# At most two of the first scatter's stores on their way, where four were allowed

## The reference

```python
xn = _layernorm(x)
x = x + _L0_gnn_ref(xn, edge_index, edge_weight, ...) + _L0_mix_ref(xn[None], ...)[0]
x = x + _L0_ffn_ref(_layernorm(x)[None], ...)[0]
xn = _layernorm(x)
x = x + _L1_gnn_ref(xn, src, dst, deg_isqrt[:, None], ...) + _L1_mix_ref(xn[None], ...)[0]
x = x + _L1_ffn_ref(_layernorm(x)[None], ...)[0]
```

## Time and profile before

| What | us |
|---|---|
| median of the timed runs | 6407.51 |
| span of the recorded execution, first to last instruction | 7249.7 |
| TensorE (PE) busy in it | 5328.2 |
| GpSimd (POOL) busy in it | 3860.9 |
| GpSimd, the 1564 stores of both scatters | 1589.6 |
| GpSimd, the 1760 gathers | 1718.7 |

### The profile page before, as it was taken

How to read it: one execution, slowest core, us unless ns; L and a number is a source line. 1 busy time by engine, 2 the same in 40 slices (tenths; PEclk the granted TensorE clock), 3 DMA queues, 4 the chain that set the end, 5 groups by cost and what they waited for, 6 DMA issues and landing times.

```text
span 7249.7 us, 87859 instructions
## 1 busy us (share of the span) xinstructions
PE 5328.2 (73%) x24977; PEld 4445.0 (61%) x24977; DVE 3382.5 (47%) x9891; ACT 1308.8 (18%) x2962; POOL 3860.9 (53%) x4349
## 2 busy tenths in 40 slices
PE   0111110667659999999899999979999899997794
PEld 0000000556537777777678887868788778876682
DVE  8511100666645555555464464436444554446323
ACT  0000000111101111111142242214111231111240
POOL 0777776000055555555888888830666326654205
PEclk9755555778779999999999999989999999999895
DMA  1000000221133333335310011021333223353223
GB/s 37 9 12 12 12 12 11 73 66 58 59 105 98 96 99 100 98 97 93 49 48 18 14 40 34 20 70 48 91 95 97 76 71 107 108 93 109 89 94 117
DMA packets 319771, 477.56 MB, mean 66 GB/s; under 512 B 99008, under 2 KB 240054, under 8 KB 319470
## 3 DMA queue, kind: packets, MB, share of 16 engines
q0 software_dynamic: 153136, 262.81, 14.8%
q1 hardware_dynamic: 166334, 211.17, 9.5%
HBM read 371.27 MB, written 102.33 MB: 65 GB/s over the span
## 4 chain that ended last, share of the span: by engine, by line
PE 57%; another core or an unknown queue 13%; DVE 11%; issue 11%; DMA 4%; DVEq 2%; ACT 1%; SPq 1%; POOL 1%; ACTq 0%; POOLq 0%
PE bank L2277 13%; PE bank L2288 13%; PE bank L2505 5%; PE bank L2338 5%; PE bank L2487 4%; PE bank L2323 4%; PE bank L2774 3%; PE bank L2630 2%; PE bank L2268 2%; PE bank L2816 1%; DMA sb_work_QT<-scratch_q 1%; DMA sb_rows<-scratch_xn,sb_row_of 1%; DMA sb_work_XC<-in_x 1%; DVE sb_STATE L1391 1%
## 5 line engine op out<-in xcount | busy, mean ns | idle before, releaser
L995 POOL DMA_INDIRECT sb_rows<-scratch_xn,sb_row_of x1760 | 1718.7, 977 | 1553.2 <-PE bank L2323 619.1
L988 POOL DMA_INDIRECT scratch_sorted<-sb_FREE x1564 | 1589.6, 1016 | 546.5 <-issue 379.2
L2288 PE MATMUL bank<-sb_work_FT,sb_W 128*128 128x250 f32 x4400 | 1006.9, 380 | 19.6 <-ACT sb_work_FT L1075 15.1
L2288 PEld LDWEIGHTS bank<-sb_work_FT,sb_W 128*128 128x128 f32 x4400 | 845.3, 193 | 134.6 <-ACT sb_work_FT L1075 22.0
L1075 ACT ACTIVATE sb_HT<-bank,sb_cols 128x250 f32<-128x250 f32 x1333 | 552.8, 467 | 2047.2 <-PE bank L2487 811.6
L2277 PE MATMUL bank<-sb_W,sb_HT 128*125 128x256 f32 x4000 | 894.2, 380 | 1.1 <-ACT sb_HT L1075 1.1
L2277 PEld LDWEIGHTS bank<-sb_W,sb_HT 128*125 128x125 f32 x4000 | 752.7, 188 | 115.4 <-ACT sb_HT L1075 1.9
L2277 PE MATMUL bank<-sb_W,sb_work_FT 128*125 128x256 f32 x1600 | 409.3, 406 | 449.8 <-issue 378.3
L2277 PEld LDWEIGHTS bank<-sb_W,sb_work_FT 128*125 128x125 f32 x1600 | 315.0, 201 | 518.0 <-issue 450.5
L2323 PE MATMUL bank<-sb_rows,sb_work_TM 128*125 128x257 f32 x1760 | 444.8, 392 | 91.2 <-issue 29.7
L1660 DVE TENSOR_TENSOR sb_FREE<-sb_FREE,bank 125x257 f32 x440 | 186.1, 423 | 698.0 <-PE bank L2323 455.1
(11 more groups left out here) (375 smaller groups left out, 7606.2 us busy)
## 6 DMA issues: line engine op xcount, KB each, us to landing
sb_rows<-scratch_xn,sb_row_of POOLq DMA_INDIRECT x1760
scratch_sorted<-sb_FREE POOLq DMA_INDIRECT x1564
scratch_qT<-sb_work_QF SPq DMA_DIRECT2D x100, 250.0 KB
sb_work_QF<-scratch_qT SPq DMA_DIRECT2D x100, 250.0 KB
sb_work_XC<-in_x SPq DMA_DIRECT2D x50, 250.0 KB
sb_work_ZT<-scratch_xn SPq DMA_DIRECT2D x50, 250.0 KB
sb_W<-in_L_mix_W SPq DMA_DIRECT2D x9, 1024.0 KB
sb_work_XC<-scratch_zs SPq DMA_DIRECT2D x28, 256.0 KB, 2.6
```

The source lines that it names most:

```text
L988: nc.gpsimd.indirect_dma_start(out=sorted_d[e], out_offset=bass.IndirectOffsetOnAxis(ap=pos[e][0:n, c:c + 1], axis=0), in_=rec[e][0:n, 2 * ...
L995: nc.gpsimd.indirect_dma_start(out=rows[:, t % RING, 0:D], out_offset=None, in_=table, in_offset=bass.IndirectOffsetOnAxis(ap=row_of[:, t: ...
L2288: ins = nc.tensor.matmul(dst[:, b, :], w[:, k0 + k, 128 * (b0 + b):128 * (b0 + b) + 128], source[:, k, :], start=(n == 0), stop=(n == 2 * ...
```

## The change

The limit becomes one for each scatter: two stores on their way in scatter 0, four in scatter 1. The semaphores that are counted up and the counts that are waited for follow from it. `PACED` stays 0.

```diff
 PACED = 0
 FLYING = 4
+FLYING_OF = (2, FLYING)
...
         def all_scattered(e):

-            return [(scattered[e][h], 16 * ((EC - h + FLYING - 1) // FLYING)) for h in range(FLYING)]
+            n = FLYING_OF[e]
+            return [(scattered[e][h], 16 * ((EC - h + n - 1) // n)) for h in range(n)]
...
-                if c >= FLYING:
-                    pool.wait_ge(scattered[e][c % FLYING], 16 * (c // FLYING))
+                if c >= FLYING_OF[e]:
+                    pool.wait_ge(scattered[e][c % FLYING_OF[e]], 16 * (c // FLYING_OF[e]))
...
-                    in_=rec[e][0:n, 2 * c:2 * c + 2], in_offset=None).then_inc(scattered[e][c % FLYING], 16)
+                    in_=rec[e][0:n, 2 * c:2 * c + 2], in_offset=None).then_inc(scattered[e][c % FLYING_OF[e]], 16)
```

## The result

The changed kernel takes 6607.34 us (median of 4 runs, 6603.01 to 6620.09), the kernel before 6406.42 us on the same chip: a ratio of 1.0311, 95% interval 1.0296 to 1.0325. It is 200.9 us slower. The forecast said slower by 72 us with a range up to 6570, so the sign was right and the size was not.

What follows compares the result with a forecast made beforehand. The later of B0's end and scatter 0's end, plus what follows, was taken as the bound. 70 delayed stores (88 us) less 10 us already waited made 78; less slack, 72: 6407.5 + 72 = 6480 us, range 6385 to 6570.

Steps and rivals of the forecast that it cites:

- The stall is the recording's: Phase A0: 854.8 us of stall in SP's loads belong to the recording; timed runs take about 27 us a pair.
- Scatter 0 ends with B0, at some 1162 to 1175 us: Before the expert weights' issue: scatter 0 ends with B0 or some us behind it, so its delay shows.
- It costs nothing in quiet stretches: Scatter 0 without traffic beside it: waiting for the store two places ahead adds no time, 1.263 us a store.
- the 1.56: Scatter 0 at limit two: 1.56 us from the end of the store two ahead to a store's own start.
- the rival in which every store waits: Scatter 0: semaphores rise late in quiet stretches too, so all stores wait; slower, 6575 us, chance 0.08.
- 120 us and half of 78: Sum behind 6575 us: 120 us for waits of all stores, on top of half of the traffic's cost.
- A store beside traffic lands 2.18 us after its end: Scatter 0 beside 100 GB/s or more: landing time taken from the first gather, giving 1.65 us a store.
- 376 us of traffic, 70 stores left over, 10 us of waits at four already: A0 and B0: 298 stores fit at 1.263 us, 228 at 1.65; 88 us less 10, net 78 us.
- Hidden anyway: Scatter 0 ends well before B0 in timed runs, so its delay falls into the gap; same, 6407 us, chance 0.23.
- Stores yield: A0 beside scatter 0: fewer stores give the loads back some 36 us; faster, 6372 us, chance 0.22.
- The recorded span of about 7265 us: Profiled run of the changed kernel: only some six pairs of A0 beside the scatter, so 15 us longer.

Runs made afterwards that it cites:

- e4: Changed kernel with a limit of eight instead of two stores on their way in scatter 0: 6333.55 us, ratio 0.9892 to the kernel before.
- e1: Changed kernel with limit four and the last 280 of scatter 0's 782 stores left out: 6274.56 us, ratio 0.9804 to the kernel before.
- e8: The kernel before, unchanged at limit four, recorded a second time: median 6411.55 us, recorded span 6409.8 us.
- e5: Changed kernel, limit two, SP's 125-partition transfers in A0 and B0 split at partition 112: 6443.45 us, ratio 1.0047 to the kernel before.

## Why the prediction was wrong

*The stall is the recording's.* Right. Two further recordings have pairs of 27.6 us beside the stores, against the 169.4 us of the earlier trace rows and the 26.93 that I took.

*Scatter 0 ends with B0, at some 1162 to 1175 us.* Wrong, and this is the first step that failed: 6407.5 - (7249.7 - 2016.7) = 1174.5, "if all behind it runs as recorded". It didn't run as recorded. From the issue of the expert weights to the end the first recording took 5233.0 us, the second one 6409.8 - 1314.64 = 5095.2. These 138 us too much put the point 138 us too early. Of them 119 lie behind the first gather (7249.7 - 2042.87 = 5206.8 against 6409.8 - 1322.21 = 5087.6); why is open. The other 19 are VectorE's work between B0 and the gathers, which the scatter hides when it ends last. The agreement that I trusted, 854.8 us of stall against 842.2 us of difference, came about by chance: the recording had the 138 us more, and lacked the 153 us for which SP waits for scatter 0 behind B0 in a timed run, because its scatter was hidden.

I had also worked out 1242 from the recorded mean pace, and passed over it. In e4, where no store waits for another, the last store starts at 1242.9; the waits at four add 69 us, which makes the 1311.6 of the kernel before. e1 shows the slip by itself: 128 us to be had at four.

*It costs nothing in quiet stretches.* Right: 1.29 us a store behind B0 at a limit of two, where the median from issue to landing is 2.1 us, that is 1.1 us after the store's end and within the 1.56. That excludes the rival in which every store waits, though its 6575 us lies nearer to the result than my forecast. (Its terms, 120 us and half of 78, give 6566.)

*A store beside traffic lands 2.18 us after its end.* Wrong, and this is the mis-sized term: 5.25 us in the mean of the five stores that were waited for beside the pair shown. I had the right row: the store of the earlier trace rows that landed 6.2 us after its end was an ordinary one. I set it aside since only four waits were recorded. But a limit of four lets a landing of up to 4 x 1.263 - 0.96 = 4.1 us pass without a wait, and few transfers stood beside that scatter (11 GB/s from 260 to 600 us, where the second recording has 74); rare waits said nothing of the landing. The gather of the earlier trace rows was no stand-in. The 125 GB/s that I put beside it are the mean of a stretch of 100 us. While it landed, from 2043.87 to 2046.05, the engines moved little but gathers (queue, packets, MB, share of 16 engines):

```profile
q0 software_dynamic: 62, 0.19, 30.8%
q1 hardware_dynamic: 2, 0.00, 0.2%
```

SP's transfers are on the second of these queues. So 2.18 us was a landing with no such transfers beside it.

*376 us of traffic, 70 stores left over, 10 us of waits at four already.* The measured count is 158 stores between two and four. With 5.25 us my own sum gives (0.96 + 5.25) / 2 = 3.1 us a store, 121 of 298 in 376 us, 177 x 1.263 = 224 us against no waits at all, where e4 shows 271. The length was too short as well: I counted slices of 100 GB/s or more, but the stores issued at 399.07 and 401.53 landed 6.6 us late while 55 to 122 GB/s were moved. And what waits at four already is 69 us and not 10. So 271 - 69 = 202.

*The rivals.* Hidden anyway is excluded by e1 and e8: there is no slack at four, there is a lag of 153 us. Stores yield is excluded by the equal GB/s (74 and 60) and ends of B0 (last `r` issued from 1131 to 1133 us on) at two, four and eight. (A quarter of that rival's 178 us is 45 and not 36; nothing hangs on it.) The recorded span of about 7265 us did not come, since it assumed that the stall would be recorded again.

## What to carry to other kernels

How many small transfers may be on their way is set by landing time over spacing, and the landing time is the one beside the traffic of that stage: here up to 9.1 us from issue to landing over 1.26 us from store to store, so four was already short and eight was enough. A limit that is rarely reached in a profile says that landings stay below its cover, not that they are short. Before a duration is used for another operation, the traffic of the very microseconds in which it was taken has to be read, and not the mean of a stretch around it. And when a recording differs from the timed runs, record it again before taking it apart, since two errors can close a sum.

## What the runs showed of the hardware

A recording can be longer than the timed runs in more than one place, and the next one can be free of it: 7249.7 us once, 6409.8 us for the same kernel later, with 119 us more in the first behind the first gather, far from the visible stall.

A small indirect store lands later beside transfers at 112 GB/s and a share of 0.3 (3.6 to 6.7 us after its end, changed kernel) than beside transfers at some 240 GB/s and a share of 0.8 (2.2 to 2.7 us, e5).
